# Three pairs of PSUM banks in turn in the rank stages of a graph network kernel, with the small uses in the same ring

## What is computed

```python
def _top_p_attention(X, W1, W2, W3):
    q = X @ W1.T @ W2.T
    k = X @ W3.T
    probs = softmax(q @ k.T)
    # keep the largest of each row until their sum reaches 0.9
    A = probs * mask
    return A / A.sum(-1, keepdims=True)

R = S + eye(N);  R = R / R.sum(-1, keepdims=True)
Z = 0; Xf = X; Xa = X
for n in range(2):
    A = _top_p_attention(Xa, W1, W2, W3)
    Xf = R @ Xf                  # the "flow"
    Xa = A @ Xa
    Z = Z + Xf @ U1[n].T + Xa @ U2[n].T
out = layernorm(X + layernorm(X + Z) * ln_g + ln_b)
```

## Time and profile before

| | |
|---|---|
| median of 3 runs | 1704.95 us (1703.96 to 1706.72) |
| the profiled execution | 1699.12 us, of which span 1697.3 |
| PE busy | 1510.8 us, 89% |
| DVE busy | 1276.6 us, 75% |
| ACT busy | 793.7 us, 47% |
| POOL busy | 260.1 us, 15% |
| mean granted clock of PE | 0.950 |
| logits, line 947: idle before it | 45.1 us, of which 42.8 released by ACT's exponential |
| maxima, line 1901: idle before it | 77.7 us, of which 69.2 released by PE's logits |

### The profile page before, as it was taken

The page is one execution under the profiler, slowest core; times in us unless marked ns, Lnnn a source line. Parts: engine busy times, 40 slices in busy tenths (PEclk is TensorE's granted clock), DMA queues, the critical chain, the costliest instruction groups (busy, mean ns, idle before and its releaser), DMA issues. The chain is left out here.

```text
span 1697.3 us, 20889 instructions
## 1 busy us (share of the span) xinstructions
PE 1510.8 (89%) x6169; PEld 838.4 (49%) x6169; DVE 1276.6 (75%) x3742; ACT 793.7 (47%) x1261; POOL 260.1 (15%) x299
## 2 busy tenths in 40 slices
PE   6999799879999999997999999989248889899996
PEld 3555345434555555553555444545225445455553
DVE  5888588823677777776899999998868788787564
ACT  4555456522556555564444444443233335444444
POOL 1011111232000000000011111112220142212312
PEclk8999899989999999997999999999669999899998
DMA  6567456654445555555555766663000000000000
GB/s 230 181 174 154 144 152 154 183 209 137 174 174 193 204 204 204 190 186 193 199 130 193 187 165 192 166 159 105 1 4 1 1 8 7 1 7 7 7 7 13
DMA packets 53463, 212.12 MB, mean 125 GB/s; under 512 B 22464, under 2 KB 31232, under 8 KB 32880
## 3 DMA queue, kind: packets, MB, share of 16 engines
q1 hardware_dynamic: 49872, 210.61, 39.8%
q0 software_dynamic: 3488, 0.31, 0.2%
HBM read 206.64 MB, written 4.50 MB: 124 GB/s over the span
## 5 line engine op out<-in xcount | busy, mean ns | idle before, releaser
L1901 DVE MAX8 cand<-banks 128x8 f32<-128x256 f32 (+1 forms) x640 | 372.5, 584 | 77.7 <-PE banks L952 51.6
L1362 ACT ACTIVATE banks<-banks,umax 128x1024 f32<-128x1024 f32 x256 | 278.7, 1089 | 312.7 <-DVE umax L1890 311.8
L929 PE MATMUL psO<-adj_in,xf 64*128 64x512 f32 x512 | 243.8, 600 | 0.0
L931 PE MATMUL banks<-adj_in,xf 64*128 64x512 f32 x512 | 243.8, 599 | 0.0
L1161 PE MATMUL psO<-ebuf,xn 128*128 128x512 f32 x512 | 241.4, 593 | 0.5 <-DVE ebuf L2110 0.5
L2110 DVE SCALAR_TENSOR_TENSOR ebuf<-ebuf 128x1024 f32<-128x1024 f32 x128 | 156.6, 1224 | 109.9 <-PE psO L1161 93.0
L1524 ACT ACTIVATE ebuf<-banks 128x1024 f32<-128x1024 f32 x128 | 130.5, 1021 | 189.3 <-PE banks L1207 162.2
L947 PE MATMUL banks<-kA,mq 64*128 64x512 f32 x256 | 166.6, 651 | 45.1 <-ACT banks L1362 42.8
L1473 ACT ACTIVATE ebuf<-banks 128x1024 f32<-128x1024 f32 x128 | 130.9, 1023 | 129.3 <-PE banks L1128 128.9
L929 PE MATMUL psO<-adj_in,xn 64*128 64x512 f32 x384 | 187.9, 600 | 0.0
L931 PE MATMUL banks<-adj_in,xn 64*128 64x512 f32 x384 | 187.9, 600 | 0.0
(11 more groups left out here) (374 smaller groups left out, 2945.0 us busy)
## 6 DMA issues: line engine op xcount, KB each, us to landing
adj_in<-in_adjT SPq DMA_DIRECT2D x128, 1024.0 KB, 5.1
adj_in<-in_adj SPq DMA_DIRECT2D x32, 2048.0 KB, 7.9
xaT<-in_xT SPq DMA_DIRECT2D x4, 512.0 KB, 5.3
xa_dram<-xa SPq DMA_DIRECT2D x8, 256.0 KB, 8.5
out<-t SPq DMA_DIRECT2D x8, 256.0 KB, 2.3
list_dram<-ids,place POOLq DMA_INDIRECT x64
rel_prob<-cut_dram SPq DMA_DIRECT2D x32, 2.0 KB
cut_dram<-ncut SPq DMA_DIRECT2D x16, 2.0 KB
```

Of the source, the lines that this page charges most:

```text
L929: low_rows = nc.tensor.matmul(psO[:], fs[0:DA, j, :], adj_in[0:DA, r % RING, j % JQ, :], start=(j == 0), stop=(j == JT - 1))
L931: high_rows = nc.tensor.matmul(psO_odd, fs[DA:P, j, :], adj_in[DA:P, r % RING, j % JQ, :], start=(j == 0), stop=(j == JT - 1))
L1362: nc.scalar.activation(ps, ps, ACT.Exp, bias=umax[:, bass.ds(i * UB + k, 1)], scale=1.0, accum_out=usum[:, bass.ds(i * UB + k, 1)]).then_i ...
L1901: last = v.max(cand[:, t % 2, at + c * 8:at + c * 8 + 8], chunk)
```

## The change

- Logits units take three pairs of banks in turn: 2 and 3, 4 and 5, 0 and 1.
- Queries (from block 1 on), rows (flows 0 to 4), z terms and ranks (of all blocks but the last) leave the shared bank and take turns in the same ring, each in the first bank of a pair. `ring_order` writes the order down; every use waits for the one three turns back (`ring_free`): a logits unit is free at its exponential, a query at ACT's copy, rows at ACT's copy, z terms at DVE's `z_rows`, ranks at `st_tally`.
- `psO_odd` moves from bank 5 to the bank of `psT`.
- `ranks` stands behind unit 10, not 12. The query stands ahead of unit 13, not 14. `z_rows` stands behind units 4 and 9, not 5 and 10.
- ACT copies the whole query into SBUF as well (`q_in`), and its last quarter and DVE's `q_lo` read that.
- The last k unit takes banks 0 and 1, and so waits for the first `k_dve`, not the second.
- Block 0 of stage 1 gets the parts of the others: two from unit 1 on, where it had none before unit 2 and three in units 7 to 10.
- `join_flow(2)` stands ahead of `add_self(3)` and `list_rows(2)`.
- At the end of stage 1 PE waits for the copy of the last flow (`r_o_sb`) before the first tile's transpose, not before the third unit of its logits.

The helpers `rows_bank`, `ranks_bank` and `z_terms_in` stand in the programs of PE, ACT and DVE alike (shown once), and replace `psT`, `psS` and `z_pair` in `to_rows`, `z_terms`, `ranks`, `rows_copy`, `other_copy`, `z_rows` and `place_step`; ACT's exponential and DVE's maxima take `ring_pair` for `unit_banks`.

```diff
@@ -129,6 +129,7 @@
         oT = sb("oT", [D, BI])
+        q_in = sb("q_in", [P, BI])
         yn = sb("yn", [P, TB, D])
...
@@ -279,18 +280,13 @@
         psO = pb("psO", [P, BI])
-        psO_odd = banks[:, 5, :]
-        def unit_banks(w):
-            first = 2 * ((w + 1) % 2)
-            return first, first + 1
...
         psT = pb("psT", [P, TB, D])
+        psO_odd = psT[:].rearrange("p t d -> p (t d)")
         psQ = psT[:].rearrange("p t d -> p (t d)")
...
@@ -394,7 +390,36 @@
-            return ((0, 1), (4, 5), (2, 3), (4, 5))[u]
+            return ((0, 1), (4, 5), (2, 3), (0, 1))[u]
+        Z_AT, RANKS_AT, QUERY_AT = (3, 8), 10, UB - 3
+        def ring_order(s):
+            order = []
+            for i in range(NB):
+                for k in range(UB):
+                    if k == QUERY_AT and i < NB - 1:
+                        order.append(("query", i + 1))
+                    order.append(("logits", i * UB + k))
+                    if s == 0 and i * UB + k in ROWS_AT:
+                        order.append(("rows", ROWS_AT[i * UB + k]))
+                    if s > 0 and i > 0 and k in Z_AT:
+                        order.append(("z", 2 * (i - 1) + Z_AT.index(k)))
+                    if i > 0 and k == RANKS_AT:
+                        order.append(("ranks", i - 1))
+            return order
+        ORDERS = [ring_order(s) for s in range(STEPS)]
+        TURNS = [{use: n for n, use in enumerate(order)} for order in ORDERS]
+        def ring_pair(s, *use):
+            first = 2 * ((TURNS[s][use] + 1) % 3)
+            return first, first + 1
+        def ring_bank(s, *use):
+            return banks[:, ring_pair(s, *use)[0], :]
...
@@ -687,14 +712,14 @@
                 SELF_BEFORE = {0: (0, 1), 1: (2,), 2: (3,), 4: (4,), 5: (5,)}
-                JOIN_BEFORE = {0: 0, 1: 1, 3: 2, 4: 3, 5: 4, 7: 5}
+                JOIN_BEFORE = {0: 0, 1: 1, 2: 2, 4: 3, 5: 4, 7: 5}
                 if s == 0:
                     for i in range(NB):
-                        if i in JOIN_BEFORE and i >= 3:
+                        if i in JOIN_BEFORE and i >= 2:
                             join_flow(JOIN_BEFORE[i])
...
                             add_self(a)
-                        if i in JOIN_BEFORE and i < 3:
+                        if i in JOIN_BEFORE and i < 2:
                             join_flow(JOIN_BEFORE[i])
...
@@ -858,6 +883,16 @@
+                def rows_bank(i):
+                    return ring_bank(s, "rows", i) if i < FLOWS - 1 else psQ
+                def ranks_bank(i):
+                    return ring_bank(s, "ranks", i) if i < NB - 1 else psS
+                def z_terms_in(i, h):
+                    bank = ring_bank(s, "z", 2 * i + h) if i < NB - 1 else psQ
+                    return bank.rearrange("p (e w d) -> p e w d", w=2, d=D)
...
@@ -873,7 +908,7 @@
                         if u == NU - 1:
-                            pe.wait_ge(g["k_dve"], 2)
+                            pe.wait_ge(g["k_dve"], 1)
                         k_unit(g, u)
...
@@ -917,7 +953,24 @@
                 def rank_q(i):
-                    nc.tensor.matmul(psQ, wq[:], xaT[:, cols(i)], start=True, stop=True).then_inc(g["r_q_ps"], 1)
+                    nc.tensor.matmul(ring_bank(s, "query", i), wq[:], xaT[:, cols(i)], start=True, stop=True).then_inc(g["r_q_ps"], 1)
+                def ring_free(*use):
+                    n = TURNS[s][use]
+                    if n < 3:
+                        return
+                    kind, which = ORDERS[s][n - 3]
+                    if kind == "logits":
+                        pe.wait_ge(g["r_exp_done"], which + 1)
+                    if kind == "query":
+                        pe.wait_ge(g["r_q_hi"], which + 1)
+                    if kind == "rows":
+                        pe.wait_ge(g["r_n_sb"], which + 1)
+                    if kind == "z":
+                        pe.wait_ge(g["r_z_sb"], which + 1)
+                    if kind == "ranks":
+                        pe.wait_ge(g["st_tally"], which + 1)
...
@@ -954,7 +1007,7 @@
-                        counts = (0,) + (2,) * 8 + (3, 3) + (2,) * 5 if prev is not None else (0, 0) + (2,) * 5 + (3,) * 4 + (2,) * 5
+                        counts = (0,) + (2,) * 8 + (3, 3) + (2,) * 5
                         assert len(counts) == UB and sum(counts) == JT
...
@@ -964,39 +1017,32 @@
                             k = t * NU + u
-                            if k == UB - 2 and more:
-                                if prev is not None:
-                                    pe.wait_ge(g["st_tally"], prev + 1)
+                            if k == QUERY_AT and more:
+                                ring_free("query", i + 1)
                                 rank_q(i + 1)
-                            if i * UB + k >= 2:
-                                pe.wait_ge(g["r_exp_done"], i * UB + k - 1)
+                            ring_free("logits", i * UB + k)
                             if prev is None and k < NU:
...
                                 pe.wait_ge(g["k_pool"], max(k + 1, NU - 1) if k < 2 else NU)
-                            even, odd = unit_banks(i * UB + k)
+                            even, odd = ring_pair(s, "logits", i * UB + k)
                             two_tiles(banks[:, even, :], banks[:, odd, :], qA[:, t * P:(t + 1) * P], qB[:, t * P:(t + 1) * P],
...
                             if prev is not None:
-                                if k == slot(2, UB):
-                                    pe.wait_ge(g["r_q_lo2"], i + 1)
                                 if s == 0 and i * UB + k in ROWS_AT:
+                                    ring_free("rows", ROWS_AT[i * UB + k])
                                     to_rows(ROWS_AT[i * UB + k])
-                                if s > 0 and k == slot(3, UB):
-                                    z_terms(prev, 0)
-                                if s > 0 and k == slot(8, UB):
-                                    z_terms(prev, 1)
-                                if k == slot(12, UB):
-                                    if s == 0:
-                                        if len([n for n in ROWS_AT if n < i * UB + k]) > 0:
-                                            pe.wait_ge(g["r_n_sb"], len([n for n in ROWS_AT if n < i * UB + k]))
-                                    else:
-                                        pe.wait_ge(g["r_z_sb"], 2 * prev + 2)
+                                if s > 0 and k in Z_AT:
+                                    ring_free("z", 2 * prev + Z_AT.index(k))
+                                    z_terms(prev, Z_AT.index(k))
+                                if k == RANKS_AT:
+                                    ring_free("ranks", prev)
                                     ranks(prev)
...
                                     pe.wait_ge(loaded, 16 * LOADS)
+                                    pe.wait_ge(g["r_q_lo2"], 1)
                                 if a > 0 and i * UB + k == flow_window(a)[0] + 1:
...
@@ -1027,8 +1073,6 @@
                     if c == 0:
-                        if n == 2:
-                            pe.wait_ge(g["r_o_sb"], NB)
                         return two_tiles(psL[bank][:, 0:BI], psL[bank][:, BI:UNIT], hqA, hqB, n, g["slot_full"])
...
@@ -1040,8 +1084,8 @@
                     pe.wait_ge(g["st_hard"], i + 1)
-                    nc.tensor.matmul(psS[:, 0:TB], before[:], hard[:], start=True, stop=True)
-                    nc.tensor.matmul(psS[:, TB:2 * TB], ones[:], hard[:], start=True, stop=True).then_inc(g["st_before"], 1)
+                    nc.tensor.matmul(ranks_bank(i)[:, 0:TB], before[:], hard[:], start=True, stop=True)
+                    nc.tensor.matmul(ranks_bank(i)[:, TB:2 * TB], ones[:], hard[:], start=True, stop=True).then_inc(g["st_before"], 1)
...
@@ -1051,6 +1095,7 @@
                 else:
+                    pe.wait_ge(g["r_o_sb"], NB)
                     tile_rows(0, 0)
...
@@ -1301,7 +1356,14 @@
                     act.wait_ge(ps, i + 1)
-                    nc.scalar.copy(qA[:, first * P:last * P], psQ[:, first * P:last * P]).then_inc(sb_, 1)
+                    if i == 0:
+                        nc.scalar.copy(qA[:, first * P:last * P], psQ[:, first * P:last * P]).then_inc(sb_, 1)
+                    elif first == 0:
+                        nc.scalar.copy(qA[:, 0:last * P], ring_bank(s, "query", i)[:, 0:last * P])
+                        nc.scalar.copy(q_in[:], ring_bank(s, "query", i)).then_inc(sb_, 1)
+                    else:
+                        act.wait_ge(g["r_q_hi"], i + 1)
+                        nc.scalar.copy(qA[:, first * P:last * P], q_in[:, first * P:last * P]).then_inc(sb_, 1)
...
@@ -1373,8 +1435,8 @@
                             if prev is not None:
-                                if s > 0 and k in (slot(3, UB), slot(8, UB)):
-                                    other_copy(prev, 0 if k == slot(3, UB) else 1)
+                                if s > 0 and k in Z_AT:
```

(8 more changed lines are left out.)

35 lines of the change are left out of this document (25 added, 10 removed).

## The result

The kernel after takes 1725.65 us (median of 4 runs, 1723.1 to 1728.55) beside 1705.84 for the kernel before: ratio 1.0111, 95% interval 1.0081 to 1.0141. It is slower by some 20 us, where 17 us faster was forecast. The profiled execution has a span of 1721.3 us against 1697.3.

A forecast was written before the change was run, and what follows sets the result against it. PE was taken to pace most of stage 0, DVE to bound stage 1. Terms -14 - 4.5 + 1.6 + 2.5 - 2.5 gave -17: 1682 against the profiled 1699.1, plus 5.8 to the runs' median, 1688 us; range 1678 to 1699.

The forecast's parts named there:

- What bounds the kernel: Rank stages: PE sets the pace in stage 0 except units 5 to 12; DVE bounds stage 1, with PE close.
- Part 1: Stage 0, block 4: the earlier join_flow(2) on POOL removes PE's 11.12 us wait and the low clock; -14 us.
- Rival (c): POOL's stall only moves, or DMA is late by PE's gain; half of the block 4 gain lost, 1697; chance 0.11.
- Part 2: Start of stage 0: the last k unit and unit 2 start earlier through other banks; -4.5 us, between 1 and 6.2 gained.
- Part 3: Ring in stage 0: the query waits for DVE's tally in blocks 1 to 6, less other PE waits; +1.6 us.
- The credit of 2.8: Stage 0: PE waits in units 0 to 4 and 15 and in block 7 go, together -2.8 us.
- Part 4: Ring in stage 1: new DVE waits before units 11 and 13, old ones gone; +2.5 us, from -8 to +11.
- block 7's late join: Stage 1, block 7: a late join, for which +0.3 us in each of seven blocks was rounded up to +2.5.
- Part 5: Block 0 of stage 1: parts done before unit 2, and fewer in units 7 and 8; -2.5 us (-1.5 to -4).
- No price: Second query copy on ACT, transpose's wait, q_lo reading SBUF and SP's untouched queue were taken to cost nothing.
- Rival (b): Ring ties PE to DVE in both stages: each stall costs 1.5 us more, +28, giving 1716; chance 0.07.
- Rival (a): Third pair pays in full: PE's waits in units 4 to 9 go in both stages, -35, 1670; chance 0.12.

The follow-up runs named there:

- e1: Kernel before with only join_flow(2) moved ahead of add_self(3) and list_rows(2) on POOL: ratio 0.994, 1693.55 us.
- e10: Kernel after, unchanged, run once more on another chip: ratio 1.0085.
- e15: Kernel after with stage 1's store of the cuts as 128 runs of 16 bytes, not 512 of 4 (computes a wrong result): 0.9952, 1688.7 us.
- e8: Kernel after with stage 1's store of the cuts behind five chunk loads, and the first tile's list and fetch behind block 6's z halves: 0.9928.
- e12: Kernel of e1 (two pairs of banks, old order) with the same moves of store, list and fetch as e8: 0.9904.
- e18: Kernel of e1 with the query ahead of unit 13, ranks behind unit 10 and z rows behind units 4 and 9: 1.0065.
- e9: Kernel of e8 with ranks behind unit 11, not 10, in both stages: 0.981, 1664.0 us.
- e3: Kernel after with stage 1's store of the cuts behind five chunk loads of a block, not one, except in block 7: 0.9967, 1698.1 us.

## Why the prediction was wrong

Point by point, in its own steps:

- **What bounds the kernel.** Right for stage 1: DVE's busy time in a block did not change, and what a block lost was idle time of DVE.
- **Part 1 (-14).** Right: 13.3 in the trace of the change, 14.0 and a kernel 11.5 us faster in e1. The granted clock of block 4 is 1.00 (0.87 in the earlier trace rows). Rival (c) did not occur.
- **Part 2 (-4.5).** Right in mechanism, sized too small: -6.6, just past its bound of 6.2. DVE's first maximum was forecast near 21.3 and stands at 21.71, behind the fourth correction at 20.45.

```profile
20.45 1.23 DVE L1773 TENSOR_TENSOR kA<-banks,kA 64x1024 fp32r<-64x1024 f32 x1
21.71 1.23 DVE L1974 MAX8 cand<-banks 128x8 f32<-128x1024 f32 x1
```

- **Part 3 (+1.6).** The wait was named rightly and sized too small, and another had no term. The query of block 4 waits for the tally as said, 1.23 us where 1.0 was read off:

```profile
199.09 1.12 PE L956 MATMUL banks<-xaT,wq 128*128 128x512 f32 x2 [1.23 <-DVEq L1897]
```

  Over blocks 1 to 6 these waits are 9.1 us; the sum had 6.6 and took 2.2 off for an earlier tally. The credit of 2.8 for PE's waits before logits came about as said: they fell from 6.1 to 3.1 us. What the prediction put at nothing is the start of a flow, whose first part now waits for ACT's copy of the flow before it, 4.8 us in three blocks (1, 4 and 5), where the kernel before has no such wait of PE:

```profile
72.44 1.22 PE L982 MATMUL psO<-adj_in,xn 64*128 64x512 f32 x1 [1.95 <-ACT z L1374]
```

  The six blocks cost +8.3 in this trace, +7.7 in e10 and +7.9 in e15: inside the bounds (-6 to +9), but not where I set the term. A hold of unit 1 in block 2 (39.0 us there; 36.8 in e10 and e15) is in the +8.3, but block 6 is 1.6 us shorter in this trace than in those two, so it can't simply be taken off.
- **Part 4 (+2.5).** The two new waits were sized well: DVE 1.88 before unit 11 (of which some 0.2 was there before) and 0.73 before unit 13, forecast 1.5 and 0.7; the waits before units 4 and 9 are gone in block 1. Blocks without the hold take 48.5 (block 1) to 48.9 us (blocks 2 to 6 in e15), forecast 49. Two things failed. The large one: nothing else was let into the sum. The bounds, "from -8 to +11", were meant for waits between PE, DVE and ACT (worked out from the conditions given with them they would be about -13 and +20), and the hold is none of these; it is 32 us of the 37.3 (in e15, without it, blocks 1 to 7 take 348.5 us, +5.6). The small one, those 5.6, lies in block 7. DVE now wants the second half of z one unit earlier, behind unit 9, and POOL has add_self(7) ahead of the addition for it, waiting for a chunk of adjacency that did not come earlier. POOL, DVE and PE in the kernel after:

```profile
1190.40 1.68 POOL L655 TENSOR_TENSOR adj_in<-adj_in,ident 128x128 f32<-128x128 f32 x4 [15.68 <-DMA adj_in<-in_adjT]
1192.04 0.72 POOL L670 TENSOR_TENSOR t<-t,xn 128x256 f32<-128x256 f32 x1
```
```profile
1192.79 0.61 DVE L1879 SCALAR_TENSOR_TENSOR z<-banks,rinv,t 128x128 f32<-128x128 f32 x2 [3.45 <-POOL t L670]
```
```profile
1193.46 0.59 PE L1087 MATMUL banks<-hard,before 128*128 128x4 f32 x2 [4.13 <-DVE z L1879]
```

  For "block 7's late join" the prediction had rounded up by some 0.4 us; a moved use has to be followed past each queue that feeds it, in the last block as in the others.
- **Part 5 (-2.5).** -4.2, a little past its bound of -4: with the fewer parts, PE's steps behind units 4 to 8 are all 2.41 us.
- **No price.** Wrong here: "SP's queue is not touched" was true and beside the point. The change moved the start of a block 1.0 us nearer to the store and 1.7 us nearer to the list writes (store from -8.3, not -9.3; lists from -2.4, not -4.1), and the prediction looked at these transfers only for who reads them.
- **The rivals.** Rival (b) named the right sign and place, DVE waiting for PE at the start of what it needs, but a wrong cause: it put 1.5 us more on each wait for a statistic, and these came as forecast in stage 1 and some 0.8 us longer in stage 0. Its total, 1716, was nearer to 1725.65 than mine by luck. Rival (a): for a third pair that pays in full, the Trainium skill, "Perfetto Trace Analysis" (Matmul Optimizations), would have all eight banks used. e8 against e12 shows no gain from ring and order together (0.9928 and 0.9904), and e18 says why: the new order costs 1.7 us a block of stage 1 and 15 us in stage 0 with two pairs, and the third pair does little more than give that back. e9 against e12 shows a gain of 0.9% once ranks stand where their turn is free; how much of that two pairs would have had is not shown.
- **Sums.** Case (c), half of part 1 lost, is 1695 and not 1697. The bounds of parts 2 to 5 added as squares are 12 to 13 and not about 9, so the range should have been 1 to 3 us wider on each side. It would not have held 1725.65 either.

Without the hold the change is worth 0.9952 (e15): 8 to 10 us faster, against the 17 forecast; the difference is parts 3 and 4 (block 7). Part 1 alone gave 10 to 11.5 (e1), so the share of all the rest is about nothing, as e8 against e12 says too. The hold costs 1.0111 - 0.9952 = 1.6% or 27 us; by e10, the kernel after on another chip, 1.3% or 22 us. The step that failed is thus part 4 with its companion "No price": transfers that nobody in the sum reads were put at nothing, and through the hold they cost 22 to 27 us. That the 512 small packets make the DMA slow, and that the hold goes with the slow stretch, is shown (e15, e3); how the order of the work brings the hold on stays open.

## What to carry to other kernels

Where a change moves an engine's work in time, look at what the DMA and the queues do at that moment too, even if nobody in the sum reads it; here a store in runs of 4 bytes made 22 to 27 us. When buffers take turns in one ring, the waits that count are those of the small uses: putting them earlier ate up what the third pair gave, and moving one of them back by a single place (e9) was worth some 20 us (e8 against e9). And a wait "for PE" at an instruction whose matmuls had ended long before is a question to put to the rows ahead of everything else.
